# Swapped blocks in the loads of a blocked triangular inverse, on one Trainium2 core

## What is computed

```python
def step(Sm, inp):
    q_, k_, v_, g_, b_ = inp
    Sm = Sm * jnp.exp(g_)[..., None, None]
    kv = jnp.einsum('bhk,bhkv->bhv', k_, Sm)
    delta = (v_ - kv) * b_[..., None]
    Sm = Sm + jnp.einsum('bhk,bhv->bhkv', k_, delta)
    o = jnp.einsum('bhk,bhkv->bhv', q_, Sm)
    return (Sm, o)
```

## Time and profile before

| what | value |
|---|---|
| time, median of 3 runs | 3113.15 us (3112.46 to 3119.73) |
| the profiled execution's own time | 3111.22 us |
| its span, first to last instruction | 3109.4 us |
| busy: PE, DVE, ACT, POOL | 2949.2, 2671.0, 1935.2, 634.4 us |
| busy share of the span: PE, DVE, ACT, POOL | 95%, 86%, 62%, 20% |
| mean granted TensorE clock | 0.978 of full speed |

### The profile page before, as it was taken

The page is one execution under the profiler, slowest core; times in us unless marked ns, Lnnn a source line. Parts: engine busy times, 40 slices in busy tenths (PEclk is TensorE's granted clock), DMA queues, the critical chain, the costliest instruction groups (busy, mean ns, idle before and its releaser), DMA issues. The chain is left out here.

```text
span 3109.4 us, 79479 instructions
## 1 busy us (share of the span) xinstructions
PE 2949.2 (95%) x29096; PEld 2419.4 (78%) x29096; DVE 2671.0 (86%) x6317; ACT 1935.2 (62%) x6258; POOL 634.4 (20%) x911
## 2 busy tenths in 40 slices
PE   6999999999999999999999999999999999649998
PEld 3788888888888888888888888888888888536665
DVE  4798989898988889898989898889888888789984
ACT  4576666666767666666667666666676766533332
POOL 1121212121212121111212121112121211162320
PEclk9899999999999999999999999999999999859999
DMA  7433434333433343433343333333343333020000
GB/s 259 141 88 107 121 108 123 105 117 103 123 107 118 89 123 109 123 100 122 96 128 89 103 115 110 121 108 115 105 121 107 116 92 101 22 99 21 28 14 17
DMA packets 454952, 319.96 MB, mean 103 GB/s; under 512 B 244003, under 2 KB 407971, under 8 KB 436902
## 3 DMA queue, kind: packets, MB, share of 16 engines
q1 hardware_dynamic: 454566, 314.87, 34.1%
HBM read 247.26 MB, written 50.73 MB: 96 GB/s over the span
## 5 line engine op out<-in xcount | busy, mean ns | idle before, releaser
L1077 DVE SCALAR_TENSOR_TENSOR conv<-xb,convw,conv 128x512 f32<-128x512 f32 x768 | 591.6, 774 | 97.6 <-ACT conv L786 82.8
L569 PE MATMUL bank<-x_hi,w_hi 128*128 128x512 f32 x1024 | 429.4, 419 | 10.1 <-PEq L263 6.4
L569 PE MATMUL bank<-x_hi,w_lo 128*128 128x512 f32 x1024 | 402.9, 393 | 0.0
L569 PE MATMUL bank<-x_lo,w_hi 128*128 128x512 f32 x1024 | 400.2, 391 | 0.0
L780 ACT ACTIVATE xb<-bank 128x512 f32<-128x512 f32 x256 | 161.7, 632 | 302.5 <-PE bank L569 277.9
L581 PE MATMUL bank<-w_hi,x_hi 128*128 128x256 f32 x1024 | 303.1, 296 | 1.6 <-ACT conv L786 1.6
L581 PE MATMUL bank<-w_lo,x_hi 128*128 128x256 f32 x1024 | 289.6, 283 | 0.0
L581 PE MATMUL bank<-w_hi,x_lo 128*128 128x256 f32 x1024 | 289.6, 283 | 0.0
L1160 POOL TENSOR_TENSOR small<-small,half 128x4 f32<-128x4 f32 x64 | 64.5, 1008 | 1047.7 <-DVE small L904 1047.7
L1188 POOL COPY halo<-xb 128x12 f32<-128x12 f32 x256 | 93.3, 365 | 863.3 <-ACT xb L780 863.3
L569 PEld LDWEIGHTS bank<-x_hi,w_hi 128*128 128x128 f32 x1024 | 193.8, 189 | 47.4 <-issue 10.1
(11 more groups left out here) (266 smaller groups left out, 7644.5 us busy)
## 6 DMA issues: line engine op xcount, KB each, us to landing
x_hi<-x_hi_scratch SPq DMA_DIRECT2D x63, 1024.0 KB, 5.0
x_lo<-x_lo_scratch SPq DMA_DIRECT2D x63, 1024.0 KB, 8.2
E<-decay_scratch SPq DMA_DIRECT2D x64, 512.0 KB, 5.4
M_scratch<-M SPq DMA_DIRECT2D x128, 256.0 KB, 2.2
w_raw<-in_w_proj SPq DMA_DIRECT2D x64, 384.0 KB, 8.5
Mt<-M_scratch SPq DMA_DIRECT2D x256, 64.0 KB, 2.0
U<-Ut SPq DMA_DIRECT2D x256, 64.0 KB, 2.0
w_raw<-in_w_out SPq DMA_DIRECT2D x32, 256.0 KB, 2.9
```

The source lines that it names most:

```text
L569: mm = pe.matmul(banks[j % 2][:].rearrange("p (b t) -> p b t", b=B), lhsT=t[f"w_{p}"][:, k, j, :], rhs=t[f"x_{q}"][:, k], start=i == 0, st ...
L1077: dve.scalar_tensor_tensor(out=y3, in0=xb[:, :, i:i + C], scalar=t["convw"][:, j, i:i + 1], in1=y3, op0=ALU.mult, op1=ALU.add).then_inc(on ...
```

## The change

Mt's columns are loaded with the same swap of blocks that its rows have, so that for a mirrored unit the 64 x 64 block that the first join needs lies in one piece. That join then takes one product of 64 x 64 for a mirrored unit too, in place of two of 64 x 32. T64 grows to 128 x 8 x 64 (4 x 64 before), and holds each unit's own two 64 x 64 diagonal blocks. The sum of Tc and Y0 is written to it directly, and the transposes of it go to U directly, so both sets of four copies on DVE and the four copies of `place` on ACT are gone. In their place the sum and the transpose are each done in four instructions, one for a quarter of the partitions. The mirrored units are now built in U with swapped blocks, and ten DMAs of single 32 x 32 blocks bring them to a new tensor Uf, from which the second half of `delta` reads. Mt takes eight DMAs. The waits on `d_M` and `d_Tc` change their counts to match. The diff, without changes of a count or a name:

```diff
-            sb(attn, "T64", 128, 4, 64)
+            sb(attn, "T64", 128, 8, 64)
...
-    M_at = lambda u, here, cols: M8[here, u, cols] if u < 4 else Mt[here, u - 4, cols]
+    M_at = lambda u, here, there: M8[here, u, there] if u < 4 else Mt[here, u - 4, there]
+    odd = lambda q: slice(q % 2 * Q, q % 2 * Q + Q)
+    U_late = lambda u: U[:, u, :] if u < 4 else Uf[:, u - 4, :]
...
                 for q in range(4):
-                    sp.dma_start(Mt[rows(3 - q)], M_units[rows(q), 4:8]).then_inc(on["d_M"], 16)
+                    own = slice(0, 64) if q < 2 else slice(64, 128)
+                    sp.dma_start(Mt[rows(3 - q), :, own], M_units[rows(q), 4:8, own]).then_inc(on["d_M"], 16)
+                for q in range(2):
+                    for k in (2, 3):
+                        sp.dma_start(Mt[rows(3 - q), :, rows(5 - k)], M_units[rows(q), 4:8, rows(k)]).then_inc(on["d_M"], 16)
...
                 for q in range(4):
-                    sp.dma_start(t["U"][rows(q), 4:8], Ut[rows(3 - q)]).then_inc(on["d_Tc"], 16)
+                    for k in range(q, 4):
+                        sp.dma_start(Uf[rows(q), :, rows(k)], U[rows(3 - q), 4:8, rows(3 - k)]).then_inc(on["d_Tc"], 16)
...
         def join_a(s):
...
                 pe.matmul(x64[hi, i], lhsT=M8[lo, i, hi], rhs=T64[lo, i, :], start=True, stop=True)
-                for q in (2, 3):
-                    mm = pe.matmul(x64[at(i + 4, q), i], lhsT=Mt[hi, i, rows(q)], rhs=T64[hi, i, :], start=True, stop=True)
+                mm = pe.matmul(x64[lo, i], lhsT=Mt[hi, i, hi], rhs=T64[hi, i + 4, :], start=True, stop=True)
...
-        def place(s):
-            act.wait_ge(on["Uc"], 2 * s + 2)
-            if s:
-                act.wait_ge(on["d_Tc"], 144 * s)
-            for q in range(4):
-                act.activation(Ut[rows(3 - q), :, rows(q)], Uc[rows(3 - q), 4:8], ACT.Copy)
...
         def turn_T(s, n):
...
-            dve.transpose(Uc[:], Tc[:]).then_inc(on["Uc"], 1)
+            dve.wait_ge(on["Tc"], s + 1)
+            if s:
+                dve.wait_ge(on["TR"], 2 * s)
+                dve.wait_ge(on["d_Tc"], 240 * s)
+            for q in range(4):
+                op = dve.transpose(U[rows(q), :, rows(q)], T64[rows(q), :, odd(q)])
+            op.then_inc(on["Uc"], 1)
...
         def y_part(s, n):
...
-                dve.tensor_tensor(Tc[:], Tc[:], y8, ALU.add).then_inc(on["Tc"], 1)
+                for q in range(4):
+                    op = dve.tensor_tensor(T64[rows(q), :, odd(q)], Tc[rows(q)], y8[rows(q)], ALU.add)
+                op.then_inc(on["Tc"], 1)
                 return
...
-            for q in range(4):
-                dve.tensor_copy(T64[rows(q), :, q % 2 * Q:q % 2 * Q + Q], Tc[rows(q), q // 2 * 4:q // 2 * 4 + 4])
             dve.wait_ge(on["Y"], 2 * s + 2)
...
-            for q in range(4):
-                dve.tensor_copy(U[rows(q), 0:4, rows(q)], Uc[rows(q), 0:4])
```

More of the change, by code:

```diff
@@ L175, in gpsimd @@
         pool.memset(t["mhalf"][:], -0.5)
-        for name in ("U", "Ut", "T64", "T16"):
+        for name in ("U", "Uf", "T64", "T16"):
             pool.memset(t[name][:], 0.0).then_inc(on["zeroed"], 1)
@@ L292, in attention @@
     M8 = t["M"][:].rearrange("p b j s -> p (b j) s")
-    Tc, Uc, Xc, T64, xf, St, R, Dl, De, O, Mt, Ut = (t[n] for n in ("Tc", "Uc", "Xc", "T64", "xf", "S", "R", "Dl", "De", "O", "Mt", "Ut"))
+    Tc, Uc, Xc, T64, xf, St, R, Dl, De, O, Mt, U, Uf = (t[n] for n in ("Tc", "Uc", "Xc", "T64", "xf", "S", "R", "Dl", "De", "O", "Mt", "U", "Uf"))
     at = lambda u, q: rows(q if u < 4 else 3 - q)
-    halves = lambda u: (lo, hi) if u < 4 else (hi, lo)
-    M_at = lambda u, here, cols: M8[here, u, cols] if u < 4 else Mt[here, u - 4, cols]
+    M_at = lambda u, here, there: M8[here, u, there] if u < 4 else Mt[here, u - 4, there]
+    odd = lambda q: slice(q % 2 * Q, q % 2 * Q + Q)
+    U_late = lambda u: U[:, u, :] if u < 4 else Uf[:, u - 4, :]
     by_pair = lambda bank: bank[:, 0:256].rearrange("p (i s) -> p i s", i=4)
@@ L432, in x_part @@
                         for q in (0, 2):
-                            here = at(u, q)
-                            mm = pe.matmul(x8[at(u, q + 1), u], lhsT=M_at(u, here, rows(q + 1)), rhs=Tc[here, u, :], start=True, stop=True)
+                            here, there = at(u, q), at(u, q + 1)
+                            mm = pe.matmul(x8[there, u], lhsT=M_at(u, here, rows(q + 1)), rhs=T64[here, u, odd(q if u < 4 else 3 - q)], start=True, stop=True)
             mm.then_inc(on["X"], 1)
@@ L450, in y_part @@
                             here = at(u, q)
-                            mm = pe.matmul(y8[here, u], lhsT=Uc[here, u, :], rhs=Xc[here, u, :], start=True, stop=True)
+                            mm = pe.matmul(y8[here, u], lhsT=U[here, u, here], rhs=Xc[here, u, :], start=True, stop=True)
             mm.then_inc(on["Y"], 1)
@@ L468, in join_b @@
                 pe.matmul(u64[lo, i], lhsT=xf[hi, i, :], rhs=U[hi, i, hi], start=True, stop=True)
[L469 removed]
+                mm = pe.matmul(u64[hi, i], lhsT=xf[lo, i, :], rhs=U[lo, i + 4, lo], start=True, stop=True)
             mm.then_inc(on["UF"], 1)
@@ L494, in delta @@
         def delta(s):
-            rhs, U = R if s % NC else two("Vn", s), t["U"]
+            rhs = R if s % NC else two("Vn", s)
             for half in range(2):
@@ L504, in delta @@
                 if half:
-                    pe.wait_ge(on["d_Tc"], 144 * (s + 1))
+                    pe.wait_ge(on["d_Tc"], 240 * (s + 1))
                 for i in range(4):
                     u = 4 * half + i
-                    mm = pe.matmul(banks[4 + half][:, i * C:(i + 1) * C], lhsT=U[:, u, :], rhs=rhs[:, u // HJ, u % HJ], start=True, stop=True)
+                    mm = pe.matmul(banks[4 + half][:, i * C:(i + 1) * C], lhsT=U_late(u), rhs=rhs[:, u // HJ, u % HJ], start=True, stop=True)
                 mm.then_inc(on["TR"], 1)
@@ L689, in join_b @@
             act.wait_ge(on["UF"], s + 1)
-            act.activation(t["U"][lo, 0:4, hi], by_pair(solve_bank(1))[lo], ACT.Copy)
-            act.activation(Ut[hi, :, hi], by_pair(solve_bank(1))[hi], ACT.Copy).then_inc(on["U_done"], 1)
+            act.activation(U[lo, 0:4, hi], by_pair(solve_bank(1))[lo], ACT.Copy)
+            act.activation(U[hi, 4:8, lo], by_pair(solve_bank(1))[hi], ACT.Copy).then_inc(on["U_done"], 1)
         def read(s):
@@ L975, in turn_T @@
             if n == 0:
[L976 to L980, removed]
-            dve.transpose(Uc[:], Tc[:]).then_inc(on["Uc"], 1)
+                dve.wait_ge(on["d_Tc"], 240 * s + 80)
+                dve.transpose(Uc[:], Tc[:]).then_inc(on["Uc"], 1)
+                return
+            dve.wait_ge(on["Tc"], s + 1)
[5 more added lines that the diff above has]
+            op.then_inc(on["Uc"], 1)
         def x_part(s, n):
```

31 lines of the change are left out of this document (12 added, 19 removed).

## The result

The changed kernel takes 3199.82 us (median; 3196.56 to 3209.77), the kernel before 3113.74 on the same chip: a ratio of 1.0279, with an interval of 1.0262 to 1.0296. That is 87 us slower, where 43 were forecast, and above the range's end of 3193. The profiled execution took 3209.77 us with a span of 3208.0. It is the slowest of the four, with a mean granted clock of 0.972 where the others had 0.974 and 0.975, so that what follows from the profile is some 10 us more than the median shows.

A forecast was written before the change was run, and what follows sets the result against it. TensorE, busy 95%, was taken to set the pace in every stage, with DVE at 86%. 3111.2 us + 23.8 (solve) + 16 (`delta`) + 3 (last stage) = 3154, given as 3156 for the median; range 3119 to 3193.

The forecast's parts named there:

- `join_a`: First join on TensorE: takes 0.61 us like `join_b`, in place of 1.95, a gain of 1.34 us a stage.
- rival 4: `join_a`'s products don't run side by side: 0.7 us a stage more, 3201 us; chance 0.04.
- the price of the quarters: DVE's quarter-height instructions in the solve don't overlap: a step of 0.43 us per sum and 0.45 per transpose.
- Rival 3: DVE's quarter-height operations overlap like whole-height ones: 3094 us if the ten loads issue fast, otherwise 3112; chance 0.11.
- the schedule: Solve: four new TensorE waits, 1.76 us, outweigh `join_a`'s gain; 0.42 us longer in 48 stages, 0.23 in 16: 23.8 us.
- DVE's last transpose: End of DVE's part of the solve: comes 0.63 us later than before.
- `delta`: TensorE waits 1.0 us there for the ten loads in 16 stages, 16 us, plus 3 us in the last stage.
- rival 1: The ten loads land in time, before `delta`, at a 0.48 us issue step: 3139 us; chance 0.13.
- The DMA step: SP's queue: the ten loads issue 0.62 us apart, with bounds of 0.48 and 0.75.
- Where weights or taps come between, it is still about in time.: SP's queue behind the ten loads: M's saves are still issued about in time; no cost was added.
- rival 2: SP falls behind; loads land later, M's second save is late, then N16, `base`, Tc, `x_part`: 3191 us; chance 0.12.
- DVE's later end costs nothing: Behind the solve, DVE waits for projections anyway, so its later end adds 0 us; without that cover, 0.2 a stage.

The follow-up runs named there:

- experiment 5: Kernel before, with only the sum to Tc and the second transpose to Uc each cut into four quarter-height instructions: 3226.33 us, ratio 1.0389.
- experiment 2: Changed kernel, with six of the ten loads to Uf issued early, after Y4_read, and only four after U_done: 3149.65 us, ratio 1.0142.
- experiment 1: Changed kernel, with the output weights' loads issued before SP waits for U_done, so not directly ahead of M's saves: 3164.25 us, ratio 1.0178.
- experiment 4: Kernel before, with the output weights' two loads issued right in front of the first save of M: 3137.1 us, ratio 1.01.
- experiment 6: experiment 2 with the quarters of the sum and of the transpose in the order 1, 2, 3, 0: 3131.48 us, ratio 1.0085.
- experiment 7: experiment 6 plus the weights' loads between the six early loads to Uf and the wait for U_done: 3139.25 us, ratio 1.0083.
- Experiment 12: Changed kernel with experiment 2's early loads, whole-height sum and transpose, and the copies of before, those to U all on ACT: 3038.94 us, ratio 0.9782.
- experiment 13: Kernel before, with only the four copies of Uc to U moved from DVE to ACT's place: 3111.0 us, ratio 1.0.

## Why the forecast was half the size

**Right: `join_a`.** 0.61 us forecast and measured; rival 4 is out.

**Right: the price of the quarters.** A sum steps by 0.43 and a transpose by 0.45 (1.71 and 1.77 for four, less the last one's 0.42 and 0.43). Rival 3 is out, and experiment 5 shows that these two edits alone are 121 us.

**Right but for one step: the schedule.** From the sum's start the five events came at 1.76, 2.59, 4.69, 5.48 and 7.07 us; forecast were 1.78, 2.55, 4.69, 5.35 and 6.93. The 0.13 and 0.14 at the last two are one step: I let `turn(r, 1)` begin before Xc had ended, as in the earlier trace rows. It began 0.04 us after (1640.25, with Xc's end at 1640.21): the transposes' last quarter stands in front of Xc now, and holds it back. In experiment 2, where the solve is all that is left, the periods of types 0 to 3 are 0.78, 0.57, 0.59 and 0.28 us longer than before. The stage of the earlier trace rows is right (0.23 forecast), the others lack this step, and type 0 something besides that no run tells apart. Times 16 they make 36 us where 23.8 were forecast, and the two profiled executions differ by 36.7 us in all. By the ratio on its own chip experiment 2 is 44 us above before (39 to 49). So this term was 12 to 20 us too small, and the missing step accounts for 7 to 9 of it (48 or 64 x 0.14). DVE's last transpose ended 0.79 us later, with 0.63 forecast.

**Right in kind, a little small: `delta`.** The waits there were 21.8 us in 17 stages, with 16 and 3 forecast, so rival 1 is out. The DMA step was 0.64 us as a median, near the 0.62 taken, and 0.68 as a mean, since ten issues take 6.4 us as a rule and up to 7.6. The wait's own worth is less: experiments 1 and 2 differ by 11 us. Type 1 came out as forecast, +1.41 for +1.42, but in part by luck: 0.57 of it is the solve's (experiment 2), with 0.42 forecast, which leaves 0.84 where 1.0 was forecast.

**Wrong: "Where weights or taps come between, it is still about in time."** I asked when SP would issue M's saves, and that was nearly right (the second, which counts, in time). I didn't ask when they land. 512 KB issued on the same queue right in front of them move their landing from 2.16 to 4.45 us after the issue. Before, the same two loads lay 2.8 us ahead of M. N16, `base`, the state's output, ACT and `gate` followed, and type 0 grew by 3.17 us. Experiments 1 and 4 agree, by removing it from the one kernel and putting it into the other: 31 us each. This is rival 2's chain with another cause in front: SP's issues were not slow, the data in front was long. The rule that the Trainium skill has (DMA: Bandwidth & Descriptors, Queues, rings and completion order), that each DMA engine takes its descriptors in the order of its ring, agrees with these rows. They don't tell the engines apart, though, and no run here separates a place further back in the ring from a plain sharing of the engines' bandwidth.

**Not forecast: the clock.** At most 21 us of the profiled execution's 98.6, and 12 to 15 in the others. In experiment 1's profile seven of the nine stretches are gone, so part of it is probably inside those 31 us; but only four of the nine lay at a wait of `gate`, and with one profile for each kernel the share is not shown.

**The sum.** By the ratios: 31 us for M behind the weights, 11 for `delta`, 18 for the order of the quarters, and 26 that stay when all is repaired (experiments 1, 2, 6 and 7), each of them good to some 5 to 10 us. Set against the forecast's terms: nothing forecast for M and 31 measured, 19 for `delta` and 11 measured, 23.8 for the solve and 44 measured. Two figures of the prediction don't come out of its own working: 48 x 0.26 + 16 x 0.45 is 19.7 and not 21, and halfway from 3156 to 3094 is 3125 and not 3119. Neither would have brought 3200 into the range.

**What the change could have been worth.** The gain in `join_a` was real, and hidden twice: by the four waits in the solve and, without them, by DVE. Experiment 12 gets 1.1 (by the ratio) to 1.2 (by its periods) of the 1.34 us a stage; experiment 13 shows that the relief of DVE alone gets none of it. I had written that DVE's later end costs nothing, because DVE waits for projections anyway. That holds while TensorE sets the pace, and not for a TensorE that is 1.3 us a stage faster.

## What to carry to other kernels

When DMAs are added to a queue, follow not only when the next transfer is issued but what bulk now lies right in front of it: here a transfer that everything waited for was issued in time and landed 2 to 4 us late. An instruction of full height cut into four quarters cost four times as much here (4 x 0.43 us for 0.42), with the same elements per partition in each quarter, and the copies that it saves must be worth that on the path, not in sum. When an engine at 95% gets faster by a margin that the one at 86% had left, ask which work can leave the second engine too: each alone gave 0.6% and 0.0%, the two together 2.2%.

## What the runs showed of the hardware

- The save of M, two transfers of 256 KB each, issued right behind two loads of 256 KB each on the same queue: its second half lands 4.0 to 4.5 us after its issue on average (6.2 at the most), and after 2.2 when the way is free.
- The order of four quarter-height instructions is worth 18 us in 64 stages, by whether the last one starts in the same quarter as its full-height follower.
- In the changed kernel's profile TensorE's granted clock fell to the lower level six times at waits of 2.0 to 3.1 us, and three times after waits of 0.8 to 1.4 us.
